# The first batch's value product taken square by square over four tiles, and the order of VectorE's lows around it

## The reference

```python
x = x + _L0_xattn_ref(_layernorm(x), ctx_2048, mask_BxS2_if0, W_in, b_in, g_res, g_init)
x = x + _L0_ffn_ref(_layernorm(x), W_r, W_k, W_v, mu_r, mu_k)

# _L0_xattn_ref
h = einsum('bld,ed->ble', rmsnorm(embeds, g_res), W_in) + b_in
# u from rmsnorm(patch_embeds, g_init)[..., :512]; s[p] = a * s[p-1] + u[p]  (a scan over patches)
out = s[plug] + h            # plug: the patch of each row, from the running sum of patch lengths

# _L0_ffn_ref
xr = mu_r * x + (1.0 - mu_r) * x_prev      # x_prev: x one row earlier
xk = mu_k * x + (1.0 - mu_k) * x_prev
r = sigmoid(einsum('btc,dc->btd', xr, W_r))
k_act = square(relu(einsum('btc,dc->btd', xk, W_k)))
out = r * einsum('btc,dc->btd', k_act, W_v)
```

## Time and profile before

| | |
|---|---|
| Median of 3 runs | 763.27 us (761.37 to 763.87) |
| Profiled execution, its own time | 761.57 us |
| Its span, first to last instruction | 760.0 us |
| Busy: PE / DVE / ACT / POOL | 98% / 77% / 53% / 23% |
| Mean granted TensorE clock | 0.991 |

### The profile page before, as it was taken

How to read it: one execution, slowest core, us unless ns; L and a number is a source line. 1 busy time by engine, 2 the same in 40 slices (tenths; PEclk the granted TensorE clock), 3 DMA queues, 4 the chain that set the end, 5 groups by cost and what they waited for, 6 DMA issues and landing times.

```text
span 760.0 us, 11067 instructions
## 1 busy us (share of the span) xinstructions
PE 745.4 (98%) x3432; PEld 616.0 (81%) x3433; DVE 586.7 (77%) x1063; ACT 405.5 (53%) x666; POOL 171.7 (23%) x163
## 2 busy tenths in 40 slices
PE   7988999999999999999999999999999999999998
PEld 5866788888888888888888888888888888888887
DVE  7888996887869778696876879778696977867462
ACT  4177354754545556453754545465364655544860
POOL 6441230313131031312113131121312113130000
PEclk9999999999999999999999999999999999999999
DMA  8667371726446272633716355281634627240011
GB/s 308 172 194 187 117 200 56 206 98 154 138 112 180 69 185 104 159 135 93 205 54 162 129 137 166 79 222 56 153 125 109 193 67 192 96 125 14 1 56 56
DMA packets 51453, 100.02 MB, mean 132 GB/s; under 512 B 5134, under 2 KB 5390, under 8 KB 51388
## 3 DMA queue, kind: packets, MB, share of 16 engines
q1 hardware_dynamic: 41900, 82.46, 31.6%
q0 software_dynamic: 9216, 16.78, 13.4%
q10 hardware_dynamic: 288, 0.27, 0.1%
HBM read 64.26 MB, written 21.76 MB: 113 GB/s over the span
## 4 chain that ended last, share of the span: by engine, by line
PE 92%; DMA 4%; POOL 1%; DVE 1%; issue 1%; ACT 0%; SPq 0%; DVEq 0%; POOLq 0%
PE bank L561 29%; PE bank L562 29%; PE bank L563 29%; PE bank L697 3%; POOL ring L505 1%; DMA ring<-s_rows,patch_now 1%; DMA xt<-in_L_ffn_W_r 1%; PE bank L791 1%; DMA ring<-s_rows,patch_of 1%; DMA above<-u 1%; DMA s_rows<-scanned 1%; PE bank L770 0%; DMA ctx_rows<-in_ctx 0%; DMA lens<-in_mask_BxS_if 0%; POOL rs_a L459 0%
## 5 line engine op out<-in xcount | busy, mean ns | idle before, releaser
L505 POOL DMA_INDIRECT ring<-s_rows,patch_now x60 | 99.9, 1665 | 228.8 <-DMA s_rows<-scanned 198.1
L1136 DVE SCALAR_TENSOR_TENSOR scratch<-turned,cols,scratch 128x512 f32<-128x512 f32 x128 | 94.4, 748 | 32.0 <-ACT scratch L862 21.9
L1003 DVE TENSOR_TENSOR xr_lo<-scratch,xr_hi 128x512 fp32r<-128x512 f32 x124 | 85.1, 688 | 39.8 <-ACT xr_hi L813 38.9
L813 ACT ACTIVATE turned<-bank 128x512 f32<-128x512 f32 x64 | 33.1, 604 | 131.1 <-PE bank L697 131.1
L561 PE MATMUL bank<-wi_hi,xt_hi 128*128 128x512 f32 x256 | 101.9, 398 | 0.0
L561 PE MATMUL bank<-xk_hi,wk_hi 128*128 128x512 f32 x256 | 100.0, 391 | 1.0 <-DVE xk_lo L1003 0.6
L563 PE MATMUL bank<-wi_hi,xt_lo 128*128 128x512 f32 x256 | 100.6, 393 | 0.0
L562 PE MATMUL bank<-wi_lo,xt_hi 128*128 128x512 f32 x256 | 100.5, 393 | 0.0
L561 PE MATMUL bank<-wr_hi,xr_hi 128*128 128x512 f32 x256 | 100.1, 391 | 0.0
L562 PE MATMUL bank<-wr_lo,xr_hi 128*128 128x512 f32 x256 | 100.0, 391 | 0.0
L563 PE MATMUL bank<-wr_hi,xr_lo 128*128 128x512 f32 x256 | 99.8, 390 | 0.0
(11 more groups left out here) (148 smaller groups left out, 1267.1 us busy)
## 6 DMA issues: line engine op xcount, KB each, us to landing
ring<-in_x SPq DMA_DIRECT2D x16, 1024.0 KB, 5.2
out<-gate SPq DMA_DIRECT2D x63, 256.0 KB, 2.1
xt<-in_x_turned SPq DMA_DIRECT2D x14, 1024.0 KB, 7.2
above<-scanned SPq DMA_DIRECT2D x42, 224.0 KB, 2.7
ctx_rows<-in_ctx SPq DMA_DIRECT2D x15, 512.0 KB, 5.9
s_rows<-scanned SPq DMA_DIRECT2D x15, 256.0 KB, 2.5
above<-u SPq DMA_DIRECT2D x14, 224.0 KB, 2.7
gate<-in_L_xattn_W_in SPq DMA_DIRECT2D x4, 256.0 KB, 3.5
```

The costliest lines, as they stand in the source:

```text
L505: pool.indirect_dma_start(ring[b.slot][:, t, :], None, s_rows[:, :], bass.IndirectOffsetOnAxis(ap=rows, axis=0), compute_op=ALU.add).then_ ...
L813: return nc.scalar.activation(to, of, ACT.Copy)
L1003: return nc.vector.tensor_tensor(to, whole, high, ALU.subtract)
L1136: nc.vector.scalar_tensor_tensor(scratch[:, 2 + i % 2, :], turned[:, c, 1:S + 1], cols[:, 1 + which, c:c + 1], scratch[:, i % 2, :], ALU.m ...
```

## The change: what it does

In batch 0 the value product takes square 0 for tiles 0 to 3, then square 1 for tiles 0 to 3, and so on, in place of tiles 0 and 1 first (their last squares held back), `far(2)` and then tiles 2 and 3. `far(2)` on TensorE now comes behind all four tiles, and its inside has one wait more, for the gating of batch 0. On VectorE, in the iteration of batch 0, the third square's low moves ahead of `stats_b`, the fourth's ahead of the first scan step, the lows of x turned of batch 2 ahead of the second scan step, and `far(2)` with the count `far_over` behind the output adds. Nothing is added or left out.

```diff
--- before.py
+++ after.py
@@ -598,6 +598,8 @@
                         else:
                             if b.fixed and b.number() < 2:
                                 reached(pe, s_copied, b, 1, 1)
+                            if is_first(b, 2):
+                                reached(pe, gated, Batch(0, 0), T, T)
                             pe.wait_ge(far_u_lo, earlier * T + 1)
 
                         product(scan_bank(b)[:, :], decay_hi[:, 1, :], decay_lo[:, 1, :], u_hi[:, :], u_lo[:, :],
@@ -711,10 +713,15 @@
                     if is_last(nxt):
                         turn(nxt)
 
-                    value_product(b, 0, 0, C - 1)
-                    value_product(b, 1, 0, C - 1)
-                    value_product(b, 0, C - 1, C)
-                    value_product(b, 1, C - 1, C)
+                    if is_first(b):
+                        for m in range(C):
+                            for t in range(T):
+                                value_product(b, t, m, m + 1)
+                    else:
+                        value_product(b, 0, 0, C - 1)
+                        value_product(b, 1, 0, C - 1)
+                        value_product(b, 0, C - 1, C)
+                        value_product(b, 1, C - 1, C)
                 if is_last(b):
                     key_product(b)
                     gate_product(b)
@@ -723,7 +730,7 @@
                     value_halves(b, T - 1)
                 if new.exists(B):
                     far(new)
-                if b.exists(B) and not is_last(b):
+                if b.exists(B) and not is_last(b) and not is_first(b):
                     for t in range(2, T):
                         value_product(b, t, 0, C)
                 if nxt.exists(B) and not is_last(nxt):
@@ -1299,28 +1306,28 @@
                     statistics_b(nxt, 0)
                     statistics_b(nxt, 1)
                     ka_low(b, 1)
+                    ka_low(b, 2)
                     stats_b(nxt, 2)
+                    ka_low(b, 3)
                     scan_step(new, 0)
-                    ka_low(b, 2)
-                    ka_low(b, 3)
                     norm_b(nxt)
+                    x_lo(new, 0)
+                    x_lo(new, 1)
                     scan_step(new, 1)
                     stats_a(new)
                     scan_step(new, 2)
                     gating(b, 0)
                     gating(b, 1)
-                    x_lo(new, 0)
-                    x_lo(new, 1)
                     scan_step(new, 3)
                     add_bias(new)
-                    far(new)
-                    dve.sem_inc(far_over, 1)
                     add_out(b, 0)
                     add_out(b, 1)
                     gating(b, 2)
                     gating(b, 3)
                     add_out(b, 2)
                     add_out(b, 3)
+                    far(new)
+                    dve.sem_inc(far_over, 1)
                     return
                 if nxt.exists(B):
                     add_x(nxt, 0)
```

## The result

| | Before | Changed |
|---|---|---|
| Median | 762.68 us (20 runs, 759.57 to 765.15) | 764.38 us (20 runs, 760.87 to 766.36) |
| Ratio | | 1.0027, 95% interval 1.0015 to 1.0039 |
| Profiled execution, its own time | 761.57 us | 760.87 us |
| Its span | 760.0 us | 759.3 us |
| Mean granted clock in it | 0.991 | 0.991 |

The forecast was 762.4 us, 0.8 us less than the 763.27 us that was then known of before. The time lies in the range of 760.5 to 764.8, but it moved the other way and by more than the interval leaves to chance. The two profiled executions say the opposite of the medians: there the changed kernel is 0.7 us the faster, almost what the sum gave. So the question is what one pair of profiles hides.

What follows compares the result with a forecast made beforehand. TensorE, busy 98% of the 760.0 us span, was taken as the bound. Terms of -4.8 (TensorE earlier), +3.9 (given back waiting for VectorE) and +0.1 (clock) gave -0.8 us: 762.4 us from 763.27, range 760.5 to 764.8.

Steps and rivals of the forecast that it cites:

- the sum: Whole kernel: -4.8 + 3.9 + 0.1 = -0.8 us, giving 762.4 us from the median of 763.27.
- TensorE's part: Batch 0's value product in square order has no waits on lows; TensorE reaches batch 1's gate product 4.8 us earlier.
- fourth rival: Batch 0's value product: cycling the PSUM banks swings the clock low, +4.8 us, 768.1 us; chance 0.02.
- VectorE's list: VectorE's reordered work up to batch 1's first mix: 2.9 us later, all idle time of 0.7, 0.4 and 1.7.
- Where the two meet: Batch 1's gate product: TensorE waits for four late lows, longest 1.6 us, giving back 3.9 of 4.8 us.
- Further down: Behind batch 1's gate product: VectorE's 2.9 us shift adds no TensorE wait; second square's low near 120.8, needed at 122.3.
- third rival: Batch 1's squares' lows: picked rows slip beyond 1.5 us in hand, each further microsecond costing one; chance 0.04.
- The term of -4.8 us: Batch 0's value product: 15.69 us against 10.88 at full speed, from waits (2.63), low clock (1.7) and slower restarts.
- 1.7 us the low clock: Behind batch 0's 2.35 us value-product wait: eight matmuls at clock 0.51 took 3.51 us, a 1.7 us loss counted as recoverable.

Runs made afterwards that it cites:

- the vector part alone: Changed kernel with batch 0's value product back in tile order ahead of the far branch, VectorE's new order kept: 764.34 us, ratio 1.0019 against before.
- the runs with one part each: Changed kernel with VectorE's old order: 760.28 us, ratio 0.9975; changed kernel with the value product's old tile order: 764.34 us, ratio 1.0019.
- before_again: The kernel before, unchanged, run as a kernel of its own for a second profile: 761.92 us, ratio 0.9994.
- defer_and_mix_first: Changed kernel, two gatings and first output add before fourth scan step, other output adds behind batch 1's mixes, all eight before batch 2's x adds: 766.08 us, ratio 1.0044.

## Why the prediction was wrong

- **TensorE's part** was right in mechanism and size: all four squares' lows in time, the value product 10.89 us, the turn 10.89 us behind its start, no loss from going round the banks (fourth rival). Alone it makes the kernel faster, by 0.25%.
- **VectorE's list** was right step by step. Idle times of 0.7, 0.4 and 1.7 us were expected, 0.82, 0.31 and 1.78 came. The first mix came 22.4 us behind the start of the value product, 23.1 expected.
- **Where the two meet** was right too: four waits, the longest 0.94 us for 1.6 expected, 1.40 in the second profile. From the turn of batch 1 to batch 1's value product it took 3.3 and 3.7 us longer than before, for 3.9 expected.
- **The step that failed is "Further down"**, which put the cost of VectorE's lateness behind the gate product at nothing: at batch 1's second square the changed kernel was to have 1.5 us in hand. Before had 3.3 us there (low ended at 119.98, needed at 123.25). The changed kernel's first profile has 1.1 (121.47 and 122.55), its second profile and the vector part alone have none (0.3 to 0.4 us of waits and a value product 1.0 us longer in each), and with the four waits filled that product is 0.8 us longer. Together with the next point this turns the sign. The rows are of the kernel before (one) and of the changed kernel (two):

```profile
123.25 0.39 PE L561 MATMUL bank<-wv_hi,xr_hi 128*128 128x512 f32 x1
```

```profile
120.79 0.68 DVE L1010 TENSOR_TENSOR xr_lo<-scratch,xr_hi 128x512 fp32r<-128x512 f32 x1
```

```profile
122.55 0.39 PE L561 MATMUL bank<-wv_hi,xr_hi 128*128 128x512 f32 x1
```

I had costed this as the third rival, at 0.04, as one late chain in place of what it is: a margin so small that each execution's chance delay of the picked rows goes into the time. Taking these waits off the path gives about 1.1 us back (762.74 against the changed kernel's 764.38 and 763.33).
- **The term of -4.8 us was too large as well**, because it was read from one execution: "1.7 us the low clock" went into the sum as a thing that every execution of before pays. With nearly the same wait the second profile pays nothing, and filling the wait gains only 1.2 to 1.4 us. By that the term is 0.3 to 0.5 us smaller on the average, an estimate with a wide interval. This alone would have left a gain.
- **The sum again, with means.** Four profiles with this order on VectorE and its waits for picked rows in the old place (59.5, 60.9, 60.4, 61.6) have a mean stretch of 60.6 us, the two of the changed kernel itself 60.2. Before has 58.6 without the fall, and with the 1.2 us that keeping the clock up gains on the average, 59.8. That is +0.8 us (+0.4 with the changed kernel's own two), where the two ratios, 1.0009 and 1.0027, say 0.7 and 2.1 us. The sum has the right sign now, from few profiles; that VectorE's order is the cause rests on the runs with one part each (0.9975 and 1.0019). Whether the rest is the same margin in executions that no profile shows, a later place, or chance in the runs, stays open.
- **Clock and time point apart.** Of 32 runs of the changed kernel 12 had a mean granted clock of 0.997 or more; of 113 of before, run beside the experiments or as before_again, 6 had. The means over these runs are 0.9943 and 0.9922; one stretch as in the earlier trace rows (3.51 us at 0.51) takes 0.0023 off a mean. By this estimate the change did save nearly one such fall per execution, as it was costed to; VectorE's lateness cost more than that.

## What to carry to other kernels

A gain that is read from one profile must be split into what every execution pays (a wait in an in-order list) and what it pays by chance (the clock behind the wait); take a second profile before the second kind goes into a sum. When TensorE is moved forward by several microseconds, the engine that feeds it can lose margin at later places (here 3.3 us became 1.1 or none), and the delays that this margin used to swallow now count; what pays then is to put waits for transfers where nobody is waiting yet. An add that is moved back also moves its store, and here everything that SyncE issues behind that store.

## What the runs showed of the hardware

- The granted clock behind a wait of the same place and nearly the same length (2.35 and 2.10 us) was 0.51 in one execution and 1.00 in another. Four waits of 0.4 to 1.4 us each, close together, left it at 1.00 in each profile that has them; waits of 1.95 and 1.40 us, 2.3 us from the end of one to the end of the other (`defer_and_mix_first`), were followed by 6.1 us at 0.50.
- Adding nine 128x512 matmuls that nobody needs, in a wait of 2.1 to 2.35 us, made the kernel 1.2 us faster (ratio 0.9982, 0.9967 to 0.9996); the clock was 1.00 in their profile.
- Kernels with the same code up to 71 us reached the value product between 71.5 and 74.5 us. This scatter of 3 us is larger than the whole effect, and only the stretch behind it made single profiles comparable.
